# A row load waits for the addition five tiles in front, and three weight loads are moved ahead of a wait

## What is computed

```
h = _layernorm(x) * (1 + ca) + sa
x = x + ga * mamba2(h)                       # projection, conv, scan, gate, projection
h = _layernorm(x) * (1 + cb) + sb
gout = xt @ Wg.T
topv, topi = jax.lax.top_k(gout, 2)
w = jax.nn.softmax(topv, axis=-1)
comb = jnp.einsum('tke,tk->te', jax.nn.one_hot(topi, E), w)
g = jnp.einsum('th,efh->etf', xt, W1) + b1[:, None, :]
v = jnp.einsum('th,efh->etf', xt, W2) + b2[:, None, :]
h = jax.nn.silu(g) * v
eo = jnp.einsum('etf,ehf->eth', h, W3) + b3[:, None, :]
x = x + gb * jnp.einsum('eth,te->th', eo, comb)
```

## Time and profile before

| | us |
|---|---|
| median of 3 runs | 825.5 |
| lowest and highest | 823.67 and 825.77 |
| the profiled execution | 832.36 |
| its span | 830.5 |
| busy in it: TensorE matmul | 680.6 |
| VectorE | 559.4 |
| ScalarE | 516.8 |
| GpSimd | 462.0 |

### The profile page before, as it was taken

One profiled execution on the slowest core, in us unless ns is written; L12 is line 12 of the kernel. 1 busy time (PEld: TensorE's weight loads), 2 busy tenths in 40 slices (PEclk: granted clock), 3 DMA queues, 4 the chain that ended last, 5 costly groups with the idle time before them and its releaser, 6 DMA issues. The chain is left out here.

```text
span 830.5 us, 13734 instructions
## 1 busy us (share of the span) xinstructions
PE 680.6 (82%) x3713; PEld 518.9 (62%) x3713; DVE 559.4 (67%) x1640; ACT 516.8 (62%) x1223; POOL 462.0 (56%) x366
## 2 busy tenths in 40 slices
PE   3678899789789999998999999999966952774982
PEld 3246557556567776876787777768755731553662
DVE  2827967988986997898689978987743561231421
ACT  3784795896796899687969977886522310221320
POOL 2003004444453378757775786688687477357775
PEclk9779798999998999999999999999996967897997
DMA  5100001112013465455346444653645774857973
GB/s 186 28 0 1 1 27 32 45 52 71 33 58 102 119 168 129 105 155 125 92 105 174 107 97 103 204 104 90 180 107 120 200 204 95 202 123 149 191 169 28
DMA packets 81275, 88.86 MB, mean 107 GB/s; under 512 B 7360, under 2 KB 67696, under 8 KB 81200
## 3 DMA queue, kind: packets, MB, share of 16 engines
q1 hardware_dynamic: 54528, 61.37, 25.6%
q0 software_dynamic: 26672, 26.62, 18.0%
HBM read 54.50 MB, written 33.46 MB: 106 GB/s over the span
## 5 line engine op out<-in xcount | busy, mean ns | idle before, releaser
L457 POOL DMA_INDIRECT out<-xs x142 | 226.8, 1597 | 116.9 <-issue 53.2
L427 POOL DMA_INDIRECT rows<-payload,pos x128 | 131.6, 1028 | 68.2 <-issue 30.2
L880 DVE SCALAR_TENSOR_TENSOR xbc<-T,table,xbc 128x511 f32<-128x511 f32 (+2 forms) x192 | 141.9, 746 | 7.7 <-ACT xbc L599 3.1
L1133 DVE SCALAR_TENSOR_TENSOR xs<-FX,xs 128x128 f32<-128x128 f32 x142 | 43.1, 345 | 122.6 <-PE FX L1457 104.7
L1457 PE MATMUL FX<-wt,hid 128*128 128x128 f32 x568 | 87.8, 301 | 17.2 <-DVE hid L1125 17.2
L655 ACT ACTIVATE xt<-FX 128x256 f32<-128x256 f32 x71 | 27.0, 380 | 110.1 <-PE FX L1434 96.0
L1457 PEld LDWEIGHTS FX<-wt,hid 128*128 128x128 f32 x568 | 73.7, 203 | 26.6 <-DVE hid L1125 17.9
L648 ACT ACTIVATE sg<-FG,wt 128x256 f32<-128x256 f32 x142 | 59.3, 471 | 47.0 <-PE FG L1444 38.4
L1444 PE MATMUL FG<-xt,wt 128*128 128x256 f32 x284 | 77.6, 397 | 12.1 <-DMA wt<-in_wt 8.1
L1287 PE MATMUL T<-h,win 128*128 128x512 f32 x128 | 76.7, 698 | 12.4 <-DVE xbc L880 10.6
L1444 PE MATMUL FV<-xt,wt 128*128 128x256 f32 x284 | 78.2, 400 | 0.0
(11 more groups left out here) (207 smaller groups left out, 1343.5 us busy)
## 6 DMA issues: line engine op xcount, KB each, us to landing
wt<-in_wt SPq DMA_DIRECT2D x71, 386.0 KB
xs<-rows SPq DMA_DIRECT2D x71, 258.0 KB
x<-in_x SPq DMA_DIRECT2D x8, 512.0 KB, 4.3
out<-x SPq DMA_DIRECT2D x8, 512.0 KB
out<-xs POOLq DMA_INDIRECT x142
rows<-pad SPq DMA_DIRECT2D x8, 258.0 KB
rows<-payload,pos POOLq DMA_INDIRECT x128
gate_a<-gates SPq DMA_DIRECT2D x8, 128.0 KB, 4.3
```

The lines of the kernel that those rows point to most:

```text
L427: pool.indirect_dma_start(d["rows"], bass.IndirectOffsetOnAxis(ap=pos[:, k, n:n + 1], axis=0), payload[:, n, :], None).then_inc(scattered, 16)
L457: pool.indirect_dma_start(d["out"], bass.IndirectOffsetOnAxis(ap=xs[:, t % XSR, c, PAY - 1:PAY].bitcast(U32), axis=0), xs[:, t % XSR, c, 0 ...
L880: last = nc.vector.scalar_tensor_tensor(out=xbc[:, t, k, tap:L], in0=T[:, k, 0:L - tap], scalar=w, in1=xbc[:, t, k, tap:L], op0=ALU.mult, ...
```

## The change

Two things change, both on SyncE. From tile 41 (`NTILES - LAST - PT`) on, `load_rows(t)` waits for the landing of the addition of tile t-5, where it was t-7; the buffers stay seven. And the weight loads of tiles 49, 50 and 51 are issued in `load_rows(49)`, behind the pads and ahead of the waits for the pads, the scatters and the additions; at their old places they are left out by `load_weights_of`. There `pads_ready` is now waited for ahead of `seq_ready`.

```diff
+AHEAD = 3
...
+            def load_weights_of(t):
+                if not 0 <= t - (NTILES - LAST) < AHEAD:
+                    load_weights(t)
+
...
             def load_rows(t):
                 p = pair_of_tile(t)
-                sp_.wait_ge(seq_ready, p + 1)
                 if t == 0:
                     sp_.wait_ge(dump_set, 32)
                 if t == NTILES - LAST:
                     sp_.wait_ge(pads_ready, 1)
                     for e in range(E):
                         set_pads_of(e)
+                    for n in range(AHEAD):
+                        load_weights(t + n)
+                sp_.wait_ge(seq_ready, p + 1)
                 if t >= NTILES - LAST:
                     sp_.wait_ge(pads_set, 16 * E)
                 sp_.wait_ge(scattered, 16 * 2 * J * (p + 1))
-                landed(sp_, t - XSR)
+                landed(sp_, t - (XSR if t < NTILES - LAST - PT else XSR - 2))
...
-                    load_weights(PT * i - 29)
+                    load_weights_of(PT * i - 29)
```

## The result

| | kernel before | changed kernel |
|---|---|---|
| median | 824.59 us (823.52 to 825.77, 4 runs) | 853.85 us (853.47 to 857.0, 4 runs) |
| profiled execution | 832.36 us | 854.22 us |
| its span | 830.5 us | 852.0 us |

The changed kernel is slower: ratio 1.0363, 95% interval 1.0332 to 1.0394; the medians are 29.3 us apart. The forecast was 842.9 with a range of 832 to 852. The direction was right; the loss was put at 17.4 us, and the median lies outside the range. Four runs of the kernel before, taken beside the experiments, fell in a slower state of the chip and are left out of every comparison.

What follows compares the result with a forecast made beforehand. In the tail GpSimd's additions were taken to set the pace (3.72 us a tile), with no slack in SyncE's in-order queue at weights 58. 19.2 - 1.8 + 0 + 0 = +17.4 on 825.5 gave 842.9 us, range 832 to 852.

Steps and rivals of the forecast that it cites:

- part 1: Five-deep wait in the tail: later row loads delay weights queued behind them on SyncE, +19.2 us by addition 70.
- step a: Tile 60: row load waits for addition 55, not 53; weights 58 and addition 57 come late, +8.0 us.
- step b: Tile 62: row load waits for addition 57; weights 61 late, addition 60 8 us behind them, +10.9 us in all.
- step c: Tile 68: row load waits for addition 63; weights 66 and addition 65 come late, +18.5 us in all.
- step d: Tile 70: row load waits for addition 65; weights 69 late, addition 70 at 841.8, +19.2 us in all.
- theory G: Formed during follow-ups: five deep, two circles, through rows (13.9 us over 3 tiles) and through weights (17 us).
- Part 2: Additions 46 to 51: fewer loads beside landings 47 and 48, more beside 48 to 50, net -1.8 us.
- Part 3: Tiles 41 to 48: output 45 delayed about 15 us but covered before addition 45, 0, between -2 and +6 us.
- Part 4: Weight loads 49 to 51 issued early: row load 49 0 to +1 us later with slack, counted as 0.
- The faster rival: Every waited-for addition lands as in the quiet case, -24 + 19.2 = -4.8 us, giving 820.7; chance 0.06.
- no effect: Five-deep wait is met anyway because another wait of the same load ends later, giving 825.5; chance 0.04.
- half the loss: Shorter landings save 6 to 9 us, steps b and d lose less, giving 834.7; chance 0.09.

Runs made afterwards that it cites:

- e1: Kernel before with only the five-deep wait from tile 41 on, weight loads at their old places: 861.93 us, ratio 1.0397 to the kernel before.
- e3: Changed kernel, but with the five-deep wait starting at tile 49 instead of 41: 856.09 us, ratio 1.0325 to the kernel before.
- e5: Changed kernel, but row loads 60 and 68 keep the seven-deep wait: 851.36 us, ratio 1.0258 to the kernel before.
- e6: Changed kernel, but weights 58 and 66 issued ahead of row loads 60 and 68: 848.29 us, ratio 1.0232 to the kernel before.
- e10: Changed kernel, five deep, but from tile 52 on each tile's weights issued directly ahead of its own rows: 840.27 us, ratio 1.0177 to the kernel before.
- e7: Kernel before with weights 58 and 66 issued ahead of row loads 60 and 68: 826.45 us, ratio 0.9987 to the kernel before.
- e2: Changed kernel with the seven-deep wait put back, so the three moved weight loads alone: 826.19 us, ratio 0.9979 to the kernel before.
- e4: Changed kernel, but with the five-deep wait for tiles 41 to 48 alone: 829.23 us, ratio 1.0003 to the kernel before.
- e11: Changed kernel with the seven-deep wait and, from tile 53, rows t+1 and weights t issued in turn: 824.23 us, ratio 0.9991 to the kernel before.
- e12: Same as e11, but with the five-deep wait for tiles 41 to 53: 827.11 us, ratio 1.0026 to the kernel before.

## Why the prediction was right or wrong, point by point

**What bounds the kernel.** Right for the stretch. The pace of the additions, SyncE's queue in order, and no slack at weights 58 were the right things to read, and steps a to d are in the chain that ended last. One reading compared unlike things: the 6.6 us of a crowded landing run to the start of the next addition and so hold some 0.7 us of GpSimd's own start, the 3.95 and 3.30 us do not. Row load 55, which waits for landing 48, is issued 0.8 us after it, at 729.39; so that landing took about 5.8 us.

**The signs.** Row load 60 stands 0.9 us behind the landing of addition 55 (757.28 to 758.19), additions 47 and 48 are 5.8 us apart, and GpSimd's four waits sum to 33.2 us: as forecast. Against addition 51 row load 60 stands 11.2 us later than before, not 8, and TensorE waits 6.0 and 6.3 us for weights 58 and 66, not 10, as it first waits for the rows of 59 and 67.

**The step that failed is the sum of part 1.** It put the loss at 19.2 us with a circle that closes through weights alone, and gave nothing for the circle through the rows, too little for the way from weights to addition, and GpSimd's bare pace for the additions between. Laid on the second profile of the kernel before at row load 40, the additions of the changed kernel moved like this (us; addition start less row load 40, changed kernel less kernel before):

| addition | measured | the prediction's sum up to there |
|---|---|---|
| 51 | 113.8 - 115.4 = -1.6 | -1.8 |
| 55 | 131.8 - 130.4 = +1.5 | -1.8 |
| 57 (step a) | 149.0 - 140.5 = +8.5 | +6.2 |
| 60 (step b) | 166.5 - 153.0 = +13.5 | +9.1 |
| 65 (step c) | 197.3 - 172.9 = +24.5 | +16.7 |
| 70 (step d) | 224.3 - 195.4 = +29.0 | +17.4 |

Four things were put too small:

1. *Additions 51 to 55 were taken as unchanged (3.3 us with the 0.2 us that -1.6 differs from -1.8).* They take 18.1 us where the kernel before has 15.1 and 15.0, since addition 54 waited 3.5 us. TensorE got the rows of tile 56 late (row load 56 waits for addition 51), and the transpose of 56 stands ahead of the down projection of 54. The chain of the changed kernel has the landing of 51, the rows of 56, their transpose and that down projection:

```profile
735.48 3.90 DMA out<-xs
...
740.18 3.02 DMA xs<-rows
...
743.25 0.45 PE FX L1441 x2
...
744.52 2.00 PE FX L1464 x8
```

   Before, output 54 was written at 741.16, ahead of addition 51 (742.35). With the five-deep wait it cannot be, as it stands behind the rows of 56 and so behind the landing of 51. In TensorE's timeline:

```profile
743.25 0.44 PE L1441 MATMUL FX<-table,xs 128*128 128x128 f32 x2 [2.88 <-DMA xs<-rows]
744.45 2.07 PE L1464 MATMUL FX<-wt,hid 128*128 128x128 f32 x8
```

   GpSimd's row names a landing as the end of this wait and the chain names output 54; both came near 747.2, as row load 58, behind landing 53, goes at 747.99. But every other kernel that is five deep beyond tile 53 has the same growth (e1, e3, e5, e6, e10: 16.9 to 19.4 us from 51 to 55), and those that are not have 14.9 to 15.6. In e1 and e3 the wait before 54 ends with the output.

   This row circle is missing from the prediction, which closed its circle through weights alone. e10 shows that about half the loss needs no late weights: with the weights out of the way 14 of the 30 us in the stretch stay. How the whole divides between the two circles is not shown, as they share engines: six deep, where by theory G only the weights are late, keeps 8 of the 30.
2. *Steps b and d: 8 us from the issue of weights to the addition (2.1 and 1.8 us).* Measured are 10.1 us (776.31 to 786.36) and 9.8 (824.73 to 834.48), as long as the 9.9 of step a. The sentence "TensorE now runs at its full clock" was the mistake. At the four places TensorE had waited 5.2 to 6.3 us for weights, and the four matmuls of the first product then take 2.08 us, later ones 1.03; from 780 to 785 us the granted clock is 0.50, the lower level, 1.2 GHz. The windows from 770 to 800 us of both kernels (span, busy by engine, then clock, DMA share, GB/s) show it as well, first the changed kernel, then the second profile of the kernel before:

```profile
770.00:800.00 30.00, 22.85 (x119) 17.59 (x119) 9.10 (x25) 6.57 (x17) 17.63 (x13) 0.89 0.63 128
```

```profile
770.00:800.00 30.00, 24.65 (x136) 18.48 (x137) 10.41 (x28) 8.75 (x23) 22.27 (x15) 1.00 0.89 189
```

   The granted clock was at its upper level, 2.4 GHz, through this stretch in the second profile of before (0.94 of it in the first), and 0.89 of it on average in the changed kernel, where TensorE is busy 22.85 us of the 30 and not 24.65.
3. *Step c: additions 61 to 63 at GpSimd's pace (3.4 us up to addition 65).* From addition 60 to 63 are 13.6 us, not 11.2: GpSimd waited 1.6 us for the output of 61, and 1.4 us before 63 for something that the profile puts down to issue. (The other 1.0 us is the difference of the two profiles of before from 60 to 65, 20.9 and 19.9 us.) A stall did not leave finished tiles behind that GpSimd could work off: TensorE had stood as well, for 5.2 us before 780.52.
4. *Step d: additions 68 to 70 at 3.72 us each (2.2 us).* From 834.48 to 844.15 are 9.7 us. It is the same in the kernel before, whose second profile has for additions 68, 69 and 70:

```profile
807.35 1.56 POOL L457 DMA_INDIRECT out<-xs  x1 [0.31 <-issue]
...
813.36 1.56 POOL L457 DMA_INDIRECT out<-xs  x1 [2.60 <-DMA out<-xs]
...
817.09 1.56 POOL L457 DMA_INDIRECT out<-xs  x1 [0.30 <-issue]
```

   Addition 69 waits for a landing in both kernels. The prediction had only the last of the three rows, and compared a time before that holds this wait with a time after that did not.

Step a comes out a microsecond smaller than forecast (7.0 between additions 55 and 57, not 8.0), mostly by the choice of the profile: the changed kernel takes 17.2 us there, the forecast had 17.4, and the two profiles of before have 9.4 and 10.2. From 65 to 70 they differ by 0.2 us. 3.3 + 2.1 + 1.8 + 3.4 + 2.2 - 1.0 - 0.2 = 11.6, which is 29.0 less 17.4.

**Part 2, -1.8 us**: the -1.6 in the table agrees, but by luck. Two profiles of before differ by as much there (addition 51 stands 117.0 and 115.4 us after row load 40), and e7, the same as before up to weights 58, has 113.9, about as the changed kernel. Nor does the nearer spacing come from the deeper wait. From addition 47 to 51 are 26.6 us in the changed kernel and 29.6 to 30.0 in those three profiles; but e2, e4 and e11, with seven deep in the tail and the weights moved, have 27.3 to 27.7, and e1, five deep with the weights in place, has 31.0. It goes with the moved weight loads, and it did not show in the times (e2: 0.9979, 0.9953 to 1.0004). Landings were also shifted more than shortened: in the changed kernel those of 48, 49 and 50 take 3.35, 4.25 and 5.12 us in the chain, where 49 took 3.95 before.

**Part 3, nothing from tiles 41 to 48**: right (e4: 1.0003), and the case that gave 6 us more to it is excluded. Addition 45 started 72.0 us after row load 40, in the two profiles of before 72.9 and 70.9. The mechanism held too: output 45 came 70.6 us after row load 40 where it was 56.6, 14 us later (15 were forecast), and addition 45 now waits 4.6 us for it, with no slack left.

**Part 4, nothing from the moved weights**: right with the seven-deep wait (e2). With the five-deep wait they save up to 6 us at addition 49 (one profile of each kernel), which the prediction did not see, as it weighed them beside the old wait only.

**The step from the profile to the median** was sound, since the sum was of differences in the tail. But the first profile was a long one: against the profile the loss looks like 21.9 us (854.2 less 832.4), of which 27 us is the tail and -5.5 us the part ahead of it.

**The faster rival and the rule behind it.** The Trainium skill says on "DMA: Bandwidth & Descriptors", in "Latency and other measured facts", that a lighter load makes the fixed cost of a transfer smaller. Addition 48 does start sooner after 47 in every kernel that is five deep there (5.8 to 6.0 us, where it is 8.1 to 8.6 in the kernel before and 6.9 to 7.0 with the weights moved and seven deep), which agrees in direction; but the later gaps take it back, and e12 shows none of it in the time. The other rivals (no effect, half the loss) were not what happened.

## What to carry to other kernels

A wait on "the result n tiles in front" closes a circle with everything that the load feeds. Write down each path from the load back to that result, the one through the rows and the one through whatever is queued behind them, divide its length by the number of tiles over which it closes, and compare with the pace of the slowest engine: here 17 us over two tiles at the worst place, and 15 us over three tiles in e10's round of the row circle, against 3.72 us a tile. When a sum is made of steps, take every duration after a new stall from rows that stand behind a stall, and lay two profiles on each other at the last point that the change does not touch before reading their difference.

## What the runs showed of the hardware that was not expected

Holding loads back changed the landings of additions very little behind tile 51. In the window from 770 to 800 us the changed kernel moved 128 GB/s where the kernel before moved 189, but the landings in its chain still took 3.24 to 3.74 us from the start of a tile's second instruction, where the earlier trace rows have 3.30 and 3.95. The crowded landings ahead of 51 moved: 48 landed in 3.35 us where it had taken 5.8, but 50 took 5.12 where it had taken about 3.6.

Executions of the kernel before differ by more than a small change is worth: 819.5 to 830.5 us in 23 runs on one chip, and the part ahead of row load 40, with the same instructions, differed by 3.7 us between two of its profiles. The profile of e11 (span 814.3) would alone have suggested a gain that its 12 times do not show.
